# Last products of a state-space stage moved to VectorE, its output gate and projection in halves, and the residual norm summed by TensorE

## What is computed

```python
def step(h, inp):                       # along the 36 tokens of a sequence
    dA_t, dBx_t, C_t = inp
    h = dA_t * h + dBx_t                # 256 channels x 16 states
    y_t = jnp.einsum('bdn,bn->bd', h, C_t)
    return (h, y_t)
...
y = jnp.moveaxis(ys, 0, 1) + x * D_param
y = y * jax.nn.silu(z) @ W_out
res = y + x_in                          # x_in = layernorm(h)
mu = jnp.mean(res, axis=-1, keepdims=True)
var = jnp.var(res, axis=-1, keepdims=True)
return (res - mu) * jax.lax.rsqrt(var + LN_EPS) * ln_g + ln_b
...
h = h + _L1_attn_ref(_layernorm(h, axis=-1), ...)
h = h + _L1_ffn_ref(_layernorm(h, axis=-1), ...)   # four experts, all of them for every token
```

## Time and profile before

| what | us |
|---|---|
| median of 3 runs (lowest, highest) | 737.35 (736.1, 740.23) |
| the profiled execution: its own time | 739.14 |
| its span in the profile | 737.3 |
| TensorE busy | 674.5 (91% of the span) |
| VectorE busy | 343.1 (47%) |
| ScalarE busy | 256.1 (35%) |
| GpSimd busy | 143.9 (20%) |

### The profile page before, as it was taken

How to read it: one execution, slowest core, us unless ns; L and a number is a source line. 1 busy time by engine, 2 the same in 40 slices (tenths; PEclk the granted TensorE clock), 3 DMA queues, 4 the chain that set the end, 5 groups by cost and what they waited for, 6 DMA issues and landing times.

```text
span 737.3 us, 15971 instructions
## 1 busy us (share of the span) xinstructions
PE 674.5 (91%) x6442; PEld 524.1 (71%) x6489; DVE 343.1 (47%) x1036; ACT 256.1 (35%) x638; POOL 143.9 (20%) x112
## 2 busy tenths in 40 slices
PE   8998899899866698998989989999999998999997
PEld 6666688795433356885755678988886556998996
DVE  3328650005999876568667632211117661211114
ACT  0433354453633505573792212222210212222221
POOL 2000100002199900120061321111100050111110
PEclk9999999999999999999999999999999999999999
DMA  8990099915465230000003889999346056899923
GB/s 305 390 339 1 16 333 381 384 69 218 148 148 147 73 129 1 0 1 1 0 2 123 320 293 338 382 348 367 124 172 271 1 193 216 339 372 352 368 93 104
DMA packets 30196, 144.97 MB, mean 197 GB/s; under 512 B 4592, under 2 KB 14640, under 8 KB 23600
## 3 DMA queue, kind: packets, MB, share of 16 engines
q1 hardware_dynamic: 26352, 136.31, 50.5%
q0 software_dynamic: 2624, 6.71, 2.6%
q10 hardware_dynamic: 1152, 0.98, 0.4%
HBM read 133.19 MB, written 10.79 MB: 195 GB/s over the span
## 4 chain that ended last, share of the span: by engine, by line
PE 72%; DVE 12%; issue 6%; ACT 5%; DMA 3%; POOL 1%; SPq 0%; DVEq 0%; ACTq 0%; POOLq 0%
PE PS L595 68%; DVE arena L2238 5%; PE PS L654 2%; DMA y_slots<-arena 1%; PE PS L618 1%; DMA arena<-bc_scratch 1%; POOL arena L1652 1%; DMA arena<-w_tok 1%; ACT XT L1261 1%; DVE stats L1714 1%; DVE arena L2369 0%; PE PS L1052 0%; ACT arena L1563 0%; ACT arena L1561 0%; DVE arena L2365 0%
## 5 line engine op out<-in xcount | busy, mean ns | idle before, releaser
L595 PE MATMUL PS<-arena 128*64 128x64 f32 (+4 forms) x3090 | 249.7, 265 | 10.1 <-DVE arena L2348 2.2
L595 PEld LDWEIGHTS PS<-arena 128*64 128x64 f32 (+1 forms) x3090 | 211.6, 155 | 38.9 <-issue 15.2
L2001 DVE TENSOR_TENSOR arena<-arena,PS 128x384 f32<-128x384 f32 (+1 forms) x66 | 26.9, 407 | 177.1 <-ACT arena L1305 177.1
L595 PE MATMUL PS<-warm 128*128 128x512 bf16 (+2 forms) x306 | 74.6, 352 | 4.9 <-POOL warm L1592 1.3
L1305 ACT ACTIVATE arena<-PS 128x384 f32<-128x384 f32 (+1 forms) x66 | 27.2, 413 | 137.0 <-PE PS L595 137.0
L1635 POOL DMA_INDIRECT y_tok<-arena,yto x32 | 29.7, 928 | 197.3 <-ACT arena L1322 90.5
L1652 POOL TENSOR_TENSOR arena<-arena 128x1152 f32<-128x1152 f32 x16 | 56.4, 3523 | 31.6 <-DVE arena L2238 31.6
L595 PE MATMUL PS<-arena,ident 128*128 128x512 f32 (+1 forms) x128 | 38.0, 440 | 21.5 <-POOL arena L1652 21.5
L595 PE MATMUL PS<-arena,wsh 128*64 128x64 f32 (+3 forms) x680 | 51.4, 251 | 5.4 <-ACT arena L1297 2.9
L595 PEld LDWEIGHTS PS<-warm 128*128 128x128 bf16 (+1 forms) x353 | 31.8, 101 | 33.2 <-issue 4.8
L1622 POOL DMA_INDIRECT x_slots<-XHW,posu x25 | 24.2, 967 | 153.6 <-DVE posu L1915 146.9
(11 more groups left out here) (319 smaller groups left out, 935.7 us busy)
## 6 DMA issues: line engine op xcount, KB each, us to landing
arena<-w_moe SPq DMA_DIRECT2D x24, 2176.0 KB, 10.2
arena<-w_moe SPq DMA_DIRECT2D x9, 2052.0 KB, 13.9
wsh<-w_moe SPq DMA_DIRECT2D x8, 2176.0 KB, 9.9
arena<-bc_scratch SPq DMA_DIRECT2D x32, 288.0 KB, 3.7
wsh<-w_moe SPq DMA_DIRECT2D x3, 2052.0 KB, 12.7
wx<-w_moe SPq DMA_DIRECT2D x1, 2176.0 KB, 18.8
wx<-w_sh SPq DMA_DIRECT2D x1, 2176.0 KB, 9.6
arena<-x_slots SPq DMA_DIRECT2D x2, 1032.0 KB, 5.5
```

Of the source, the lines that this page charges most:

```text
L595: return nc.tensor.matmul(out_, l, r, start=start, stop=stop, skip_group_check=True)
L2001: ins = v.tensor_tensor(firsts(hid_b[x][:, 0:full], n_), firsts(sg_s[x][:, 0:full], n_), firsts(PS[:, 2 * x + 1, 0:full], n_), ALU.mult)
```

## The change

- The products by C of the last state (15, counting from 0) and of half 1 of state 14 go from GpSimd to VectorE, as single halves (`times_C`), between the last two scans and behind them. GpSimd's last three products (states 12, 13 and half 0 of state 14) leave its loop; each now also waits until VectorE's next product by B is done (`dbx_done`).
- `Y_PARTS` is put in another order (half 0, then half 1), TensorE's loop ends after state 13, and for the last two states it waits piece by piece. Idle products (L1014) go.
- The gate is multiplied in three parts: half 0, the two tails, half 1. The first two projections (tiles 0 and 1, half 0) run before half 1 is there.
- The statistics of `TMP` are taken pair by pair behind each pair's addition. `ln_b` is added to `H` by GpSimd, before the scans.
- `root * TMP + H` and its five instructions on VectorE go: TensorE adds identity times `H` and diagonal times `TMP` in PSUM (`ACCS`), ScalarE writes the diagonals (`dg`), and VectorE takes the second statistics and `XH` from PSUM and copies the sum to `H` behind that.
- `keep_warm(12)` becomes two times `keep_warm(1)` and one idle product. One warming operand in the transposes moves to another bank.

```diff
+        def ACCS(j):
+            return PS[0:TILE_N[j], (7, 4, 5)[j // 2], (j % 2) * D:(j % 2 + 1) * D]
...
-            with pe.Fori(0, NS // 2) as i:
+            with pe.Fori(0, NS // 2 - 1) as i:
...
-            idle_products(7)
-            pe.wait_ge(sem("ys_ready"), 1)
-            token_products("attn1", lambda k, j: ys[:, k, tsl(j)], KD, lambda k: wout_s[:, k, :])
-            keep_warm(12, root=6)
+            pe.wait_ge(sem("hc_done"), NS + 1)
+            for i, (d, ts, acc) in enumerate(Y_PARTS):
+                if i == 2:
+                    pe.wait_ge(sem("ys_ready"), 1)
+                last = mm(acc, ident[:, :], hC[:, 0, d, ts], False, False)
+            last.then_inc(sem("hc_read"), 1)
+            for i, (d, ts, acc) in enumerate(Y_PARTS):
+                if i in (0, 2):
+                    pe.wait_ge(sem("ys_ready"), 2 + i // 2)
+                last = mm(acc, ident[:, :], hC[:, 1, d, ts], False, True)
+                if i != 1:
+                    last.then_inc(sem("hc_read"), 1)
+            pe.wait_ge(sem("ys_ready"), 5)
+            for j in range(2):
+                mm(TM(j), ys[:, 0, tsl(j)], wout_s[:, 0, :], j == 0, False)
+            pe.wait_ge(sem("ys_ready"), 6)
+            for j in range(NT - 1):
+                for k in range(1 if j < 2 else 0, KD):
+                    last = mm(TM(j), ys[:, k, tsl(j)], wout_s[:, k, :], k == 0, k == KD - 1)
+                last.then_inc(sem("tm_ready"), 1)
+            last_tile_products(lambda k: ys[:, k, tsl(NT - 1)], lambda k: wout_s[:, k, :], KD)
+            pe.wait_ge(sem("bias_step"), 3 + len(PAIRS))
+            for q, (j0, n) in enumerate(PAIRS):
+                if q:
+                    pe.wait_ge(sem("ys_ready"), 6 + q)
+                for j in range(j0, j0 + n):
+                    mm(ACCS(j), ident[0:TILE_N[j], 0:TILE_N[j]], tile(H, j), j == j0, False)
+            keep_warm(1, 3, root=5)
+            idle_products(1, 3)
+            for j in range(NT):
+                pe.wait_ge(sem("ys_ready"), 11 + j + (j > 0))
+                pe.wait_ge(sem("z_silu"), 2 + j)
+                mm(ACCS(j), dg[0:n_, j, 0:n_], tile(TMP, j), False, True).then_inc(sem("hc_read"), 1)
+            keep_warm(1, 3, root=6)
...
+            act.wait_ge(sem("ys_ready"), 12)
+            for j in range(NT):
+                nc.scalar.activation(dg[0:n_, j, 0:n_], ident[0:n_, 0:n_], ACT.Copy, scale=root[0][0:n_, j, 3:4])\
+                    .then_inc(sem("z_silu"), 1)
...
+            pool.wait_ge(sem("xh_ready"), NT * (SUB["attn1"] + 1))
+            for q, (j, n) in enumerate(PAIRS):
+                g.tensor_tensor(pair(H, q), pair(H, q), row("ln_b")[0:TILE_N[j], None, :].to_broadcast([TILE_N[j], n, D]), ALU.add)\
+                    .then_inc(sem("bias_step"), 1)
...
+            def times_C(i, n, half=4):
...
+                d = slice(0, half - 2)
+                nc.gpsimd.tensor_tensor(hC[:, n % 2, d, :], hs_[:, n % 2, d, :],
+                                        bcC[:, n:n + 1, :].to_broadcast([128, half - 2, T]), ALU.mult)\
+                    .then_inc(sem("hc_done"), 1)
...
+            for n in range(3):
+                pool.wait_ge(sem("dbx_done"), min(NS - 1 + n, NS))
+                times_C(NS // 4 - 1, n, 4 if n < 2 else 3)
...
+            def times_C(n, d):
+                dve.wait_ge(sem("scan_half"), 2 * n + d + 3)
+                dve.wait_ge(sem("hc_read"), n + 1)
+                dve.wait_ge(sem(f"C{n % 4}"), 16 * (n // 4) + 16)
+                v.tensor_tensor(hC[:, n % 2, d, :], hs_[:, n % 2, d, :], bcC[:, n % 4, :], ALU.mult).then_inc(sem("ys_ready"), 1)
...
+            dve.wait_ge(sem("dbx_done"), NS)
+            dve.wait_ge(sem("hc_done"), NS)
+            half_scan(NS - 1, 0)
+            times_C(NS - 2, 1)
+            half_scan(NS - 1, 1)
+            times_C(NS - 1, 0)
+            times_C(NS - 1, 1)
...
+            for q in range(len(PAIRS)):
+                tile_in(3 * NT, 2 * q)
+                if q < len(PAIRS) - 1:
+                    v.tensor_tensor(pair(TMP, q), TM2(q), pair(XH, q), ALU.add).then_inc(sem("ys_ready"), 1)
...
+                for j in range(PAIRS[q][0], PAIRS[q][0] + PAIRS[q][1]):
+                    tile_stats(tile(TMP, j), j)
+            variances()
+            half_variance()
+            for j in range(NT):
+                if j == 1:
+                    newton().then_inc(sem("ys_ready"), 1)
+                v.scalar_tensor_tensor(tile(TMP, j), tile(TMP, j), tile(mv, j)[:, 0:1], row("ln_g")[0:TILE_N[j]],
+                                       ALU.subtract, ALU.mult).then_inc(sem("ys_ready"), 1)
+            for j in range(NT):
+                dve.wait_ge(sem("hc_read"), NS + 5 + min(2 * (j // 2) + 1, NT - 1))
+                tile_stats(ACCS(j), j)
+            variances()
+            layer_norm_h(of=ACCS)
+            for q, (j0, n) in enumerate(PAIRS):
+                mark(v.tensor_copy(pair(H, q), PS[0:TILE_N[j0], (7, 4, 5)[q], 0:n * D].rearrange("p (j d) -> p j d", d=D)))
```

More of the change, by code:

```diff
@@ L317, in tower @@
         Y_CUT = 512
-        Y_PARTS = [(0, slice(0, Y_CUT), PS[:, 0, 0:Y_CUT]), (1, slice(0, Y_CUT), PS[:, 1, 0:Y_CUT]),
-                   (0, slice(Y_CUT, T), PS[:, 2, 0:T - Y_CUT]), (1, slice(Y_CUT, T), PS[:, 2, T - Y_CUT:2 * (T - Y_CUT)])]
+        Y_PARTS = [(0, slice(0, Y_CUT), PS[:, 0, 0:Y_CUT]), (0, slice(Y_CUT, T), PS[:, 2, 0:T - Y_CUT]),
+                   (1, slice(Y_CUT, T), PS[:, 2, T - Y_CUT:2 * (T - Y_CUT)]), (1, slice(0, Y_CUT), PS[:, 1, 0:Y_CUT])]
         dBx = part(8 * U1, 2, KD, T)
@@ L621, in transpose_x @@
                         last.then_inc(sem("xt_psum"), 1)
-                    idle_products(1, {"attn2": 5, "attn3": 3}.get(name, 7), 256)
+                    idle_products(1, {"ffn1": 3, "attn2": 5, "attn3": 3}.get(name, 7), 256)
             def gate_logits(name):
@@ L1004, in _ @@
             for i, (d, ts, acc) in enumerate(Y_PARTS):
-                mm(acc, diagD[:, d, :], xs[:, d, ts], i < 3, False)
+                mm(acc, diagD[:, d, :], xs[:, d, ts], i != 2, False)
             pe.sem_inc(sem("hc_read"), 2)
             keep_warm(3)
-            with pe.Fori(0, NS // 2) as i:
+            with pe.Fori(0, NS // 2 - 1) as i:
                 for n in range(2):
@@ L1013, in _ @@
                     last.then_inc(sem("hc_read"), 1)
-            idle_products(7)
-            pe.wait_ge(sem("ys_ready"), 1)
-            token_products("attn1", lambda k, j: ys[:, k, tsl(j)], KD, lambda k: wout_s[:, k, :])
-            keep_warm(12, root=6)
+            pe.wait_ge(sem("hc_done"), NS + 1)
[30 more added lines that the diff above has]
+                pe.wait_ge(sem("z_silu"), 2 + j)
+                n_ = TILE_N[j]
+                mm(ACCS(j), dg[0:n_, j, 0:n_], tile(TMP, j), False, True).then_inc(sem("hc_read"), 1)
+            keep_warm(1, 3, root=6)
             transpose_x("ffn1")
@@ L1466, in _ @@
             nc.scalar.activation(zs[:, :, :], zs[:, :, :], ACT.Silu).then_inc(sem("z_silu"), 1)
-            xt_copy("ffn1", norms=2)
+            inverse_root()
+            act.wait_ge(sem("ys_ready"), 12)
+            for j in range(NT):
+                n_ = TILE_N[j]
+                nc.scalar.activation(dg[0:n_, j, 0:n_], ident[0:n_, 0:n_], ACT.Copy, scale=root[0][0:n_, j, 3:4])\
+                    .then_inc(sem("z_silu"), 1)
+            xt_copy("ffn1")
             gate_exp("ffn1")
@@ L1644, in _ @@
                     .then_inc(sem(f"row0{j}"), 16)
+            pool.wait_ge(sem("xh_ready"), NT * (SUB["attn1"] + 1))
+            for q, (j, n) in enumerate(PAIRS):
+                g.tensor_tensor(pair(H, q), pair(H, q), row("ln_b")[0:TILE_N[j], None, :].to_broadcast([TILE_N[j], n, D]), ALU.add)\
+                    .then_inc(sem("bias_step"), 1)
             pool.sem_inc(sem("hc_done"), 2)
-            with pool.Fori(0, NS // 4) as i:
-                for n in range(4):
[L1649 to L1654, removed]
+            def times_C(i, n, half=4):
+                pool.wait_ge(sem("scan_half"), 8 * i + (2 * n + half))
+                pool.wait_ge(sem("hc_read"), 4 * i + (n + 1))
+                pool.wait_ge(sem(f"C{n}"), 16 * i + 16)
+                d = slice(0, half - 2)
+                nc.gpsimd.tensor_tensor(hC[:, n % 2, d, :], hs_[:, n % 2, d, :],
+                                        bcC[:, n:n + 1, :].to_broadcast([128, half - 2, T]), ALU.mult)\
+                    .then_inc(sem("hc_done"), 1)
+            with pool.Fori(0, NS // 4 - 1) as i:
+                for n in range(4):
+                    times_C(i, n)
+            for n in range(3):
+                pool.wait_ge(sem("dbx_done"), min(NS - 1 + n, NS))
+                times_C(NS // 4 - 1, n, 4 if n < 2 else 3)
             for e in range(E1 - 1):
@@ L2246, in _ @@
                     scan(i, n)
-            for n in range(4):
-                if n < 3:
-                    input_of(NS // 4 - 1, n + 1)
-                scan(NS // 4 - 1, n)
```

(37 more changed lines are left out.)

## The result

The changed kernel takes 732.57 us (median of 4 runs, 731.57 to 733.01), the kernel before 737.92 in the same series (736.1 to 740.23): a ratio of 0.9916, 95% interval 0.9894 to 0.9938. It is faster by 0.6 to 1.1%; the forecast was 4.2 us (0.6%), 733.2. The profiled execution took 733.01 us, its span 731.2.

What follows compares the result with a forecast made beforehand. One serial path from 259 to 281 us was taken to bound the kernel; 2.6 + 0.6 + 1.6 - 0.6 = 4.2 us off the 737.35 median gave 733.2, range 731.4 to 736.4.

Steps and rivals of the forecast that it cites:

- 2: last sum starts: Last two states, products by C on VectorE: TensorE's last sum starts at 258.4, 0.8 us earlier than before.
- 3: gate of half 1: Gate and projection: half 1's gate begins at 260.9 and takes 0.69 us instead of the whole gate's 1.5.
- 4: first aggregation: Norm's first statistics, taken by pairs in waits for TensorE: aggregation at 266.85 instead of 270.08; gives 0.6 us.
- 6: logits: Normed tiles read from PSUM, 2.34 us instead of 1.70: minus 0.6; copies to `H` fit VectorE's idle time.
- the tail: End of the state-space stage, from GpSimd's last products through gate and projection to the first addition: gain 2.6 us.
- pairs: First statistics of the norm taken behind each pair's addition, filling waits for TensorE: gain 0.6 us.
- the norm's three terms: Residual norm: statistics by pairs 0.6, sum and second statistics through TensorE 1.6, normed tiles from PSUM minus 0.6 us.
- step 5: Norm's second statistics: TensorE reaches the diagonals at 268.8, 0.3 us late; aggregation at 272.0, 4.9 earlier; gives 1.6 us.
- Step 1: State 13: GpSimd's product starts behind VectorE's product by B, losing little; ends at 254.15, 0.5 us late.
- The mechanism: Last states: GpSimd coming first holds up VectorE, up to 1.3 us on the path; gain 2.9, 734.4 us; chance 0.18.
- Two of the prediction's own signs of being wrong: Last states: a product by C on VectorE of over 1 us, and a gap between TensorE's last sums.
- The clock rival: Norm, around 272 and 273: TensorE's granted clock falls from 2.4 to 1.2 GHz, giving 743 us; chance 0.05.

Runs made afterwards that it cites:

- the copy with the delay: Changed kernel with 25 warm products ahead of the next feed-forward part's transposes, giving the saving back: 738.35 us, ratio 1.0 against the kernel before.

## Why the prediction was right

The serial path was read rightly, and its terms came out within 0.25 us. With 1.41 subtracted, for the common point (in brackets the time as the trace has it):

| step of the prediction | predicted | measured |
|---|---|---|
| 2: last sum starts | 258.4 | 258.28 (259.69) |
| 3: gate of half 1 | 260.9 | 260.75 (262.16) |
| 3: first addition | 262.8 | 262.66 (264.07) |
| 4: first aggregation | 266.85 | 266.86 (268.27) |
| 5: products by diagonals | 268.8 | 268.89 (270.30) |
| 5: second aggregation | 272.0 | 271.94 (273.35) |
| 6: logits (280.66 - 4.2) | 276.5 | 276.23 (277.64) |

Step by step: the tail was forecast at 2.6 and measured at 2.71 alone; pairs 0.6 and 0.53; the norm's three terms together 0.6 + 1.6 - 0.6 = 1.6 and 1.74. TensorE was late at the diagonals, as step 5 has it: without its warm products the path is 0.27 shorter. Copies to `H` cost nothing, as said: 1.64 us of idleness are left behind them. Nor did `ln_b` on GpSimd: from the start of the normed copy to VectorE's step at 182.74 took 5.77 us before (from 176.97) and takes 5.77 now (178.38 to 184.15).

What was sized wrongly or not seen:

- Step 1 costs the waits at "little" and asks only what they lose. They lose even less: the 0.15 us counted for VectorE's last product by B did not come (it starts at 249.82 again, 251.23 in the trace). But the prediction did not see that the unrolled products would come ahead of VectorE without the waits: 4.2 us of the 4.4 hang on them. The mechanism stood among the rivals, at up to 1.3 us, the length of the half product; its true price, for a full product, is 2.44 us each time.
- Two of the prediction's own signs of being wrong stood in the first profile. VectorE's first product by C took 1.07 us there, beside GpSimd's half product (1.40 against the 1.31 forecast), which the slow sum of state 12 had held up by 0.41. And the last sum's first weight load came 0.58 us after TensorE was free, when VectorE's product was there. Neither stands in a profile without the fall of the clock: at 1.00, in the second series' profile, the product took 0.73 and the three sums ran as one stretch of 6.76 us. The path was 34.22 there and 34.25 in the first profile, so neither cost anything.
- The clock rival had its place wrong. In the norm the clock held, but at the last sums it fell in 2 of the 3 profiles of the changed kernel, hidden in one (path 34.25) and at a price of 2.0 us in another (36.24).
- The median fell by 5.35, 5.4 and 5.7 us in three series, the path by 4.4, or 2.4 in one profile. The path accounts for 4.4 us; the further microsecond was not forecast, and its cause stays open. In the profiles it lies behind 430 us, where weights are loaded and where two executions of one kernel differ by 2 us. From the third layer's logits to the fourth's took 178.98 and 179.27 us in the kernel before and 177.86 to 178.29 in the three profiles of the changed kernel; from there to the end took 153.65 and 151.72 before, 151.41 to 151.70 in those three. But the copy with the delay took 177.11 and 153.59, so these profiles do not tie it to the change, and in the times of that copy no gain remains.

## What to carry to other kernels

When a loop is written out, look at what its overhead had ordered: two engines released by the same event keep their order only if something makes them, and a wait on the engine that can afford it cost little here. Gains on a serial path added up as long as the clock stayed at its higher level. They are best measured from one instruction to another inside a trace: the path of the kernel before repeated to 0.01 us, that of the changed kernel to 0.03 but for the one profile in which the clock fell deeper; the stretch to the end of one kernel did not repeat within 1.9 us. Judge warm products by the times and granted clocks of many runs, not by one profile.

## What the runs showed of the hardware

- VectorE's product of two operands from SBUF (128x1152) took 1.36 us alone or when it started ahead of GpSimd's, and 3.80 when it came second; GpSimd's took 2.6 alone and 3.71 when it came second. A scan that reads PSUM and SBUF shows no such effect: 2.60 for two with a GpSimd product beside them.
- In a steady loop, with TensorE busy 2.4 us of each 4, the granted clock stayed at 1.00 in both profiles of the kernel before. In the changed kernel one wait ahead of the sum of state 12 was longer, 1.76 or 1.77 us instead of 1.55. Behind it the clock fell to 0.50 in the first and third profile, and stayed at 1.00 in the second, of the same program. With ten warm products in the waits ahead of states 12 and 13 it stayed at 1.00 in both profiles taken.
